# A fused gated scan and ternary FFN on one core: VectorE and ScalarE lists in a new order

## The reference, cut to what matters

```
h  = LN(x)
u, v = split(h @ in_proj_w + in_proj_b)            # 512 + 512 columns
vl = conv3(silu(v)) + conv_b                       # depthwise, along the rows
s[t] = a * s[t-1] + ssm_b * vl[t]                  # a scan over all 8192 rows
y  = ssm_c * s + ssm_d * vl
o  = (u * silu(y)) @ out_proj_w + out_proj_b
x  = x + LN(LN(o + h) * ln_w + ln_b)               # end of the first layer
g  = gelu(LN(x) @ ternary(W1).T + b1)              # 512 -> 2048
f  = g @ ternary(W2).T + b2                        # 2048 -> 512
x  = x + LN(f)
```

## Time and profile before

| | |
|---|---|
| median of 3 runs | 1498.55 us |
| the profiled execution | 1498.6 us, span of its instructions 1496.8 us |
| mean granted TensorE clock | 0.984 of full speed |
| PE busy | 1416.4 us (95%), 9002 matmuls |
| DVE busy | 1220.6 us (82%), 2402 instructions |
| ACT busy | 913.1 us (61%), 1504 instructions |
| POOL busy | 356.5 us (24%), 522 instructions |
| DMA | 98.13 MB in all |

### The profile page before, as it was taken

One profiled execution on the slowest core, in us unless ns is written; L12 is line 12 of the kernel. 1 busy time (PEld: TensorE's weight loads), 2 busy tenths in 40 slices (PEclk: granted clock), 3 DMA queues, 4 the chain that ended last, 5 costly groups with the idle time before them and its releaser, 6 DMA issues.

```text
span 1496.8 us, 25048 instructions
## 1 busy us (share of the span) xinstructions
PE 1416.4 (95%) x9002; PEld 885.7 (59%) x9002; DVE 1220.6 (82%) x2402; ACT 913.1 (61%) x1504; POOL 356.5 (24%) x522
## 2 busy tenths in 40 slices
PE   7999999899999999999999999999999999989997
PEld 4444646457475664756657566574666747555664
DVE  7999869788797887978889698897988879898634
ACT  7997756556466564674756556575665646743543
POOL 4243321222202222131222212222122220222111
PEclk9999999999999999999999999999999999999999
DMA  8702613215122151320513304142131512202320
GB/s 248 259 30 58 166 31 76 38 29 113 29 63 51 29 113 29 85 43 15 113 28 87 55 13 103 29 100 42 44 71 29 113 29 58 29 1 57 57 29 29
DMA packets 164653, 98.13 MB, mean 66 GB/s; under 512 B 133680, under 2 KB 133680, under 8 KB 164400
## 3 DMA queue, kind: packets, MB, share of 16 engines
q1 hardware_dynamic: 155888, 80.79, 21.2%
q0 software_dynamic: 8640, 15.73, 7.4%
HBM read 31.49 MB, written 32.51 MB: 43 GB/s over the span
## 4 chain that ended last, share of the span: by engine, by line
PE 37%; DVE 30%; issue 15%; ACT 8%; POOL 3%; DVEq 0%; POOLq 0%; ACTq 0%
PE f1b L614 6%; PE f1b L613 6%; DVE bn L904 5%; PE f2b L664 4%; DVE ring L922 3%; PE misc L576 3%; PE misc L578 3%; PE misc L577 3%; PE f2b L654 3%; ACT tp L1944 3%; ACT xn L1934 2%; DVE hb L1161 2%; PE f2b L639 2%; PE f2b L637 2%; POOL rsc L2278 2%
## 5 line engine op out<-in xcount | busy, mean ns | idle before, releaser
L613 PE MATMUL f1b<-x3T,w 128*128 128x256 f16 x1792 | 400.7, 274 | 0.0
L614 PE MATMUL f1b<-x3T,w 128*128 128x256 f16 x1792 | 400.5, 274 | 0.0
L1840 ACT ACTIVATE ring<-f1b,par 128x256 f32<-128x256 f32 x480 | 201.1, 470 | 237.3 <-PE f1b L614 237.0
L2277 POOL TENSOR_SCALAR ve<-mv 128x4 f32<-128x4 f32 (+2 forms) x89 | 36.8, 414 | 797.5 <-DVE mv L914 797.3
L922 DVE SCALAR_TENSOR_TENSOR ring<-ring,f_sc 128x512 f16<-128x512 f32 x256 | 187.3, 738 | 34.8 <-ACT ring L1854 34.8
L654 PE MATMUL f2b<-w,ring 128*128 128x512 fp8e5 x768 | 197.1, 379 | 0.0
L613 PEld LDWEIGHTS f1b<-x3T,w 128*128 128x128 fp8e5 x1792 | 176.2, 98 | 24.8 <-issue 0.4
L614 PEld LDWEIGHTS f1b<-x3T,w 128*128 128x128 fp8e5 x1792 | 176.0, 98 | 24.2
L1854 ACT ACTIVATE ring<-ring,f_sc 128x512 f16<-128x512 f32 x256 | 182.2, 719 | 0.0
L576 PE MATMUL misc<-x1T,win_hi 128*128 128x512 f16 x456 | 179.4, 393 | 0.0
L577 PE MATMUL misc<-x1T,win_hi 128*128 128x512 f16 x456 | 178.6, 392 | 0.0
(11 more groups left out here) (263 smaller groups left out, 2823.4 us busy)
## 6 DMA issues: line engine op xcount, KB each, us to landing
out_dram<-xs SPq DMA_DIRECT2D x60, 256.0 KB, 2.7
xs<-x_dram SPq DMA_DIRECT2D x14, 1024.0 KB, 6.1
out_dram<-hb POOLq DMA_DIRECT2D x36, 256.0 KB, 5.4
out_dram<-stage POOLq DMA_DIRECT2D x24, 256.0 KB, 4.6
ring<-w1t_dram SPq DMA_DIRECT2D x3, 1024.0 KB, 13.1
stage<-w2t_dram SPq DMA_DIRECT2D x3, 1024.0 KB, 8.4
x1T<-tp SPq DMA_TRANSPOSE x68, 3.1
xs<-x_dram SPq DMA_DIRECT2D x4, 256.0 KB, 4.1
```

Source lines behind the costliest of these rows:

```text
L613: pe.matmul(o_, w, src[:, k, h * TH:(h + 1) * TH], start=k == 0, stop=False)
L614: mm = pe.matmul(o_, w, src[:, KC + k, h * TH:(h + 1) * TH], start=False, stop=k == KC - 1)
L1840: ins = act.activation(gg[:, i % G_SLOTS, ts], f1b[i % 2][:, ts], ACT.Gelu, bias=par[:, B1 + chunk:B1 + chunk + 1], scale=1.0 / ACT_SCALE)
```

## The change

Both engines' tables of due times are edited, some code moves inside a step, and one tile changes its kind.

- VectorE, first half: taps of chunks 2 and 3 go from 2.4, 2.45 to 2.25, 2.26, ahead of all scans; the statistics of `drain(e, 1)` go from behind the drain (0.8 and 1.15) to 2.27, between taps and scans; `lo(5)` and its sums go from 6.2, behind the last `y`s, to 4.2, ahead of them.
- ScalarE, first half: `d_conv` of chunks 2 and 3 go from 6.15 and 7.15 to 4.15 and 4.16; `ffn_norm` of the seven-product tiles moves two places back.
- Middle: the first four instructions of `drain(fa, 0)` and `h_add(c, 0)` are issued between the low parts of x, not behind them.
- Second half: `lo(9)` and `lo(11)` come earlier (9.3 and 11.65, before 10.2 and 12.2).
- Step 3: three of the eight W2 sums and the difference of b2 move ahead of the table; five are left in it, one at a place.
- `seven(t)` now excludes tile 13, which uses eight products; its end and the statistics around it are written accordingly.

The core of the diff, as far as the prediction speaks of it:

```diff
-AT_TAP0, AT_TAP2 = (1.1, 1.15, 1.4, 1.45), (1.3, 1.35, 2.4, 2.45)
+AT_TAP0, AT_TAP2 = (1.1, 1.15, 1.4, 1.45), (1.3, 1.35, 2.25, 2.26)
...
-AT_D_CONV, AT_CENTRE = (3.15, 3.16, 6.15, 7.15), (13.3, 13.5, 14.3, 14.5)
+AT_D_CONV, AT_CENTRE = (3.15, 3.16, 4.15, 4.16), (13.3, 13.5, 14.3, 14.5)
...
+AT_LO_SECOND = (9.3, 11.2, 11.65, 13.2, 14.2, 15.2, 16.2)
...
-AT_COMBINED = (7.65, 7.66, 11.65, 11.66, 14.65, 17.5, 17.51, 17.52)
+AT_F_STATS_SEVEN = 2.27
+AT_F_NORM_SEVEN = (6.15, 6.2, 7.15, 7.2)
+AT_COMBINED = (7.65, 9.25, 11.65, 14.65, 17.5)
...
-        return 1 < t < NT - 2
+        return 1 < t < NT - 3
...
+                if s == 3:
+                    combine(2, 0)
                 if n is not None:
                     run(ln1(n))
...
+                parts = drain(fa, 0) if seven(fa) else []
                 if n is not None:
-                    for j in range(NB):
-                        t_lo("t1", n, j)
+                    if s == 3:
+                        combine(0, 0)
+                    t_lo("t1", n, 0)
+                    if s == 3:
+                        combine(0, 1)
+                    t_lo("t1", n, 1)
+                    for part in parts[:3]:
+                        part()
+                    t_lo("t1", n, 2)
+                    h_add(c, 0)
+                    for part in parts[3:4]:
+                        part()
+                    t_lo("t1", n, 3)
+                    parts = parts[4:]
...
-                    parts = drain(NT - 3, 1)
-                    for part in parts[:4]:
-                        part()
+                    f_add(NT - 3, 0)
+                    f_add(NT - 3, 1)
                     h_add(NT - 1, 0)
-                    for part in parts[4:]:
-                        part()
+                    f_add(NT - 3, 2)
+                    f_add(NT - 3, 3)
```

More of the change, by code:

```diff
@@ L945, in combine @@
                 left, right = slice(0, TH), slice(TH, 2 * TH)
-                if q == 0:
+                if q == 2 and g == 0:
                     ve_.wait_ge(w_ok, NCH)
-                else:
-                    ve_.wait_ge(comb_ok, (0, g + 1, 0, 2 + g + 1)[q])
+                elif q % 2 == 1:
+                    ve_.wait_ge(comb_ok, g + (q // 2) * 2 + 2)
                 in0, in1 = ((w2[:, ps, right], w2[:, ps, left]), (w2[:, qs, right], combined[:, 0, ps, :]),
@@ L1036, in epilogue @@
                     return (spread(AT_F_ADD, .1, drain(e, 1))
-                            + spread(AT_F_STATS, .1, [lambda j=j: f_stats(e, j) for j in range(2, NB)])
-                            + spread(AT_F_AGGR, .01, [lambda j=j: aggr(4, e, j) for j in range(2, NB)]))
+                            + spread(AT_F_STATS_SEVEN, .001, [lambda j=j: f_stats(e, j) for j in range(2, NB)])
+                            + spread(AT_F_STATS_SEVEN + .004, .001, [lambda j=j: aggr(4, e, j) for j in range(2, NB)]))
                 return (spread(AT_F_ADD, .2, [lambda j=j: f_add(e, j) for j in range(NB)])
@@ L1760, in _ @@
                 if c is not None:
-                    parts = drain(fa, 0) if seven(fa) else []
                     for j in range(NB):
-                        h_add(c, j)
-                        for part in parts[2 * j:2 * j + 2]:
-                            part()
+                        if n is None or j > 0:
+                            h_add(c, j)
                         if s == NT - 1:
@@ L1773, in _ @@
                                 aggr(1, c, j - 2)
+                        for part in parts[2 * j - 2:2 * j] if j else []:
+                            part()
                     h_stats(c, NB - 1)
@@ L1783, in _ @@
                 if s == 3:
-                    works = [b2_difference] + [lambda q=q, g=g: combine(q, g) for q in range(4) for g in range(2)]
-                    items += list(zip((AT_COMBINED[0],) + AT_COMBINED, works))
+                    b2_difference()
+                    items += [(at, lambda i=i: combine(*divmod(i, 2))) for i, at in zip((2, 3, 5, 6, 7), AT_COMBINED)]
                 if s < NT - 1:
@@ L1788, in _ @@
                 if fa is not None:
-                    at_lo = AT_LO_LAST if s == NT - 1 else [j + 1.2 for j in range(half(s), FC)]
+                    at_lo = AT_LO_LAST if s == NT - 1 else AT_LO_SECOND
                     items += lows(fa, range(half(s), FC), [0] * half(s) + list(at_lo))
@@ L1816, in _ @@
                         h_stats(NT - 1, j)
-                        if j > 1:
-                            aggr(4, NT - 3, j)
+                        aggr(4, NT - 3, j)
                     for j in range(NB):
@@ L2215, in _ @@
                 if e is not None:
-                    items += [(at, lambda j=j: ffn_norm(e, j)) for j, at in enumerate(AT_F_NORM)]
+                    items += [(at, lambda j=j: ffn_norm(e, j)) for j, at in enumerate(AT_F_NORM_SEVEN if seven(e) else AT_F_NORM)]
                 if c is not None and s < NT:
```

6 lines of the change are left out of this document (2 added, 4 removed).

## The result

The changed kernel takes 1417.97 us (median of 4 runs, 1417.19 to 1419.9) beside 1498.87 us for the kernel before on the same chip: a ratio of 0.946, 95% interval 0.945 to 0.948. A second set on another occasion gave 1416.73 us (1415.89 to 1417.91), ratio 0.946 (0.944 to 0.948). The forecast was 1414, its own range 1409 to 1419. The profiled execution took 1419.9 us, with a span of 1418.1 us, where the span before was 1496.8.

A forecast was written before the change was run, and what follows sets the result against it. TensorE was taken as the bound, its unworked time being waits of order and clock falls. From 1498.6 us, 71.5 saved in tiles 2 to 12 and 13.0 in tile 13 gave 1414 us, range 1409 to 1419.

The forecast's parts named there:

- First half, third pair: Sums needed by f2(4): in time with 0.6 us to spare, so the 2.47 us wait and the clock fall go.
- Second pair: Sums needed by f2(2): the tight place, no slack; 0.15 us of wait taken per step, bounds 0 and 1.
- Rival A: Second pair of sums late, 1 us in each of 11 steps, no clock fall: 1424 us; chance 0.20.
- First pair: Sums needed by f2(0): statistics ahead of them only change places with lo(0) and the first taps; no gain counted.
- Middle: Output projection's third block: h_add(0) comes some 2.2 us earlier where 1.3 are needed, so the 1.3 us wait goes whole.
- B: One wait of 1.5 to 2.5 us stays per step, at v or the third pair, with clock falls: 1451 us; chance 0.09.
- D: At v's first block, drain parts and h_add beside GpSimd's adds delay x's low parts: slower, 1507 us at 8.5 per step; chance 0.02.
- Second half: Earlier norms and lo(9) ahead of the statistics remove the second half's small waits, 6.4 us in 22 places.
- The clock: Tiles 2 to 12: ten falls of 1.65 us, 16.4 us, behind the extra wait and nine 2.3 us waits; none behind short waits.
- First seven-product tile: Its 4.9 us wait for first sums shrinks to some 1.6 us, bounds 0 to 2.6, with no clock fall.
- Tile 13: Stretch to tile 14's first f2 falls from 110.99 to 98.0 us, 0.9 of it wait at the last gates; saves 13.0.
- The shared port: Step 3's W2 sums beside GpSimd's adds lose 0.77 us each, inside x's slack; by full exclusion up to 1.7, giving 1415 or 1416.

The follow-up runs named there:

- slack for pair two: Changed kernel with tap 3, the D product of chunk 3 and the last scan moved later, so the second pair of sums ends earlier; 1413.82 us, ratio 0.944.
- first half and middle back: Changed kernel with both the first half and the middle of a step put back to the old order; 1475.72 us, ratio 0.986 to the kernel before.
- four edits: Changed kernel with later tap, D product and scan, tile 1's statistics behind the first sums, last W2 sum moved, tile 13's lo(14), lo(15) earlier; 1410.57 us, ratio 0.942.

## Why the prediction was right, and by how much its steps were off

By the profiled execution the forecast missed 5.8 us (1419.9 against a sum of 1414.1): 3.0 before tile 2 (265.74 for 262.73), 2.2 in tiles 2 to 12 (942.73 for 940.5), 1.1 in tile 13 (99.13 for 98.0), less 0.6 behind it. That execution lies 0.9 us above the forecast's own range, the median 1 us inside it. In the second profile of the same kernel the 3.0 are absent.

*Bound and period.* Right. The wait-free step was put at 85.2 us; it is 85.07, seen in the run with slack for pair two. The kernel before was bound by TensorE plus waits of order, and VectorE's 10 idle microseconds in each step absorbed nothing.

*First half, third pair.* Right: it was to be in time with 0.6 us to spare, and has 0.77.

*Second pair.* Right in place, a little small: no slack was read, 0.15 us taken, 0.25 measured. Rival A had put it at 1 us.

*First pair.* Missed. The move of the statistics was costed at nothing, as changing places with `lo(0)`. At their old place the first pair is 0.91 us late in ten steps, some 9 us in all. The sum took this gain in unseen, since it took the wait-free step as the goal; that it came out right here was luck, not working. The profile of before had the hint, a first pair without slack. VectorE's timeline in step 10, the last sum of that pair, and TensorE's, `f2(0)`:

```profile
818.50 0.29 DVE L966 TENSOR_TENSOR stage<-ring,stage 128x256 f16<-128x256 f16 x1
```

```profile
817.78 1.03 PE L654 MATMUL f2b<-w,ring 128*128 128x512 fp8e5 x4
818.85 0.39 PE L664 MATMUL f2b<-w,ring 128*128 128x256 fp8e5 x2
```

The pair ended at 818.79, and the narrow matmul started 0.21 us behind the 817.78 + 0.86 = 818.64 at which it could have. To cost that move at nothing was the step that failed, though it did not move the sum.

*Middle.* Right: 1.3 us per step, confirmed alone at 1.34, no clock behind it. The low parts of x stayed in time; nothing in front of v waits, so B and D did not come.

*Second half.* Right that the 6.4 us go. Which of two causes, I had not separated; either is enough. But the gain is whole only with the statistics moved as well: with first half and middle back the step was 0.27 us shorter than before, not 6.4 / 11 = 0.58.

*The clock.* Right in sum, wrong as a rule. The prediction tied a fall to a wait of 2.31 us. That wait came unchanged in three kernels, eleven times each, and was followed by a fall 9, 7 and 2 times. By waits alone 4.73 x 11 = 52.0 us of the 69.3 went in tiles 2 to 12, nine falls are 14.9, the first wait 2.4.

*First seven-product tile.* Mis-sized: 1.6 us was to stay, 2.56 stayed in the profile, and behind it a fall (1.65 us) that was excluded because the wait would be short. The changed kernel run again had a wait of 2.48 us, with a fall. The 1 us that the split W2 sums were to bring did not come. VectorE's timeline at the end of step 3, then TensorE's:

```profile
259.08 1.22 DVE L955 TENSOR_TENSOR stage<-w,stage 128x1024 fp8e5<-128x1024 fp8e5 x1
...
262.85 2.46 DVE L907 BATCH_NORM_STATS2 bn<-hb 128x6 f32<-128x512 f32 x4
...
268.98 0.29 DVE L969 TENSOR_TENSOR stage<-ring,stage 128x256 f16<-128x256 f16 x1
```

```profile
269.32 0.52 PE L667 MATMUL f2b<-w,ring 128*128 128x256 fp8e5 x2 [2.56 <-DVE stage L969]
```

The clock fell at 269.45, which is why this narrow matmul takes 0.52 in place of 0.38 us. What the prediction left out are the four statistics of tile 1 (2.46 us and 0.3 for `aggr`), which keep their old place, since tile 1 is no seven-product tile.

*Tile 13.* Right in size (98.0 against 99.13, and 98.13 in the run with four edits, where the last two `lo` stand ahead of the x updates that wait for GpSimd). The wait of 0.84 us (L640 for L925) is the difference; the prediction had put its 0.9 at the last gates, where 0.3 was found.

*The shared port.* The prediction weighed 0.77 us per W2 sum beside an add, by a row, against up to 1.7. VectorE's timeline of a W2 sum beside GpSimd's add, and GpSimd's timeline (alone such a sum takes the 1.22 us of the row at 259.08):

```profile
210.46 2.29 DVE L955 TENSOR_TENSOR stage<-w 128x1024 fp8e5<-128x1024 fp8e5 x1
```

```profile
210.17 1.49 POOL L2349 TENSOR_TENSOR hb<-hb,row 128x512 f32<-128x512 f32 x1 [3.07 <-ACT hb L1916]
```

One of the two met an add: 1.07 us longer. The add had 1.20 us left when the sum began. The other sum, at 208.72, met none. That is the size of an exclusive wait for the rest of the add, not of a slowdown at a fixed rate. The Trainium skill, "SBUF — State Buffer", section "Who interferes with whom", says that the second to issue is blocked until the first ends; the rows agree with it, better than with the 0.77 that I took from an average. Nothing in front of v was late, so TensorE did not notice.

Of the 3.0 us before tile 2, 2.0 are the same thing by chance, at a place that the change leaves alone; most of the rest are longer waits of TensorE on VectorE's `wm_sq` in the first 110 us (3.2 us, where the kernel before has 2.3 and the second profile of the changed one 1.7). VectorE's and TensorE's timelines:

```profile
121.06 3.09 DVE L1410 SCALAR_TENSOR_TENSOR w<-stage,thr,w 128x512 fp8e5<-128x512 f32 x3
```

```profile
126.84 0.39 PE L593 MATMUL misc<-wo_hi,g_hi 128*128 128x512 f16 x1 [1.82 <-DVE hb L1144]
```

Three such instructions take 2.06 or 2.07 us in the thirteen other profiles, that of the kernel before among them, all with the same code here. In this one the third of them met an add of GpSimd and lost 1.0 us; so did one of the four low parts of the gate just ahead (3.75 us at 117.39, where the kernel before has 2.73). TensorE lost 1.98.

## What to carry to other kernels

A wait between two engines that both idle is one of order: follow the late operand back to the first instruction that stood in the list while its own input was long there, and move that. Then work out the slack of every other meeting point at the new pace, those that had just enough before above all; an edit that looks neutral, like the moved statistics here, can be what keeps them in time. Boundary tiles follow other branches of the code, and need the same edit made for them by hand.
